# Router gate folded into the two projections of an attention and mixture-of-experts kernel, with all attention stages in a new order

## The reference

```
x: (8, 512, 128) float32; 4096 tokens of 128 numbers
x = x + attention(layernorm(x)); x = x + experts(layernorm(x))
attention: Q, K, V = n @ W.T + b, 16 heads of 8; scores = Q K^T, causal mask, no softmax
           out = (scores * causal) V;  return out @ wo.T + bo
experts:   probs = softmax(n2 @ Wg) over 8 experts; the top 2 of each token
           y = sum over the two of p * (relu(n2 @ W1[e] + b1[e]) @ W2[e] + b2[e])
```

## Time and profile before

| | |
|---|---|
| median of 3 runs (range) | 298.18 us (297.58 to 298.75) |
| the profiled execution, its own time | 297.89 us |
| its span in the trace | 296.1 us |
| busy: PE, DVE, ACT, POOL | 228.8, 201.2, 142.4, 204.5 us |
| mean granted TensorE clock | 0.899 of 2.4 GHz |

### The profile page before, as it was taken

The page is one execution under the profiler, slowest core; times in us unless marked ns, Lnnn a source line. Parts: engine busy times, 40 slices in busy tenths (PEclk is TensorE's granted clock), DMA queues, the critical chain, the costliest instruction groups (busy, mean ns, idle before and its releaser), DMA issues.

```text
span 296.1 us, 6311 instructions
## 1 busy us (share of the span) xinstructions
PE 228.8 (77%) x1392; PEld 171.2 (58%) x1392; DVE 201.2 (68%) x696; ACT 142.4 (48%) x509; POOL 204.5 (69%) x188
## 2 busy tenths in 40 slices
PE   0499999999999998988794399999997999840000
PEld 0244666666656565655573279988996989830000
DVE  7978889889898998989967485454443544410284
ACT  3234366646476463654444156666664757510000
POOL 3166568738889889889776777777777777777000
PEclk9999999999999999999955569999999999985555
DMA  6940000000100100100115532343333333211599
GB/s 203 312 101 0 0 3 0 3 1 20 38 26 29 39 27 28 38 27 28 49 53 114 132 101 74 98 111 97 97 104 98 106 97 104 82 49 34 184 358 309
DMA packets 32357, 24.98 MB, mean 84 GB/s; under 512 B 4388, under 2 KB 30252, under 8 KB 32322
## 3 DMA queue, kind: packets, MB, share of 16 engines
q1 hardware_dynamic: 23766, 14.01, 17.8%
q0 software_dynamic: 4320, 8.47, 8.8%
q10 hardware_dynamic: 4236, 2.10, 2.4%
HBM read 13.41 MB, written 11.61 MB: 84 GB/s over the span
## 4 chain that ended last, share of the span: by engine, by line
PE 49%; DVE 16%; issue 11%; DMA 11%; POOL 5%; ACT 2%; SPq 2%; ACTq 1%; POOLq 1%; DVEq 0%
PE ps L820 15%; PE ps L790 7%; PE ps L909 6%; PE ps L917 6%; POOL returned L397 5%; DMA returned<-y_sb,xt 4%; DMA back<-returned 4%; DVE o_sb L590 3%; DVE prod L577 3%; DMA xt<-dispatched 2%; PE ps L811 2%; PE ps L829 2%; SPq L323 2%; PE ps L840 2%; PE ps L792 2%
## 5 line engine op out<-in xcount | busy, mean ns | idle before, releaser
L397 POOL DMA_INDIRECT returned<-y_sb,xt x71 | 70.2, 989 | 21.7 <-issue 17.4
L358 POOL TENSOR_TENSOR outer<-qkv 128x1024 f32<-128x1024 f32 x32 | 62.5, 1954 | 27.3 <-ACT qkv L452 26.9
L388 POOL DMA_INDIRECT dispatched<-rows,slot x64 | 62.6, 978 | 18.9 <-issue 14.5
L820 PE MATMUL ps<-outer,causal 128*128 128x512 f32 x128 | 63.1, 616 | 0.0
L766 DVE TENSOR_SCALAR y_sb<-ps,xt 128x128 f32<-128x128 f32 x71 | 24.9, 350 | 45.3 <-PE ps L919 45.3
L909 PE MATMUL ps<-xT,w_of 128*128 128x128 f32 x284 | 48.7, 295 | 1.6 <-ACT xT L502 1.1
L917 PE MATMUL ps<-w_sb,hT 128*128 x284 | 44.7, 281 | 0.5 <-DVE y_sb L766 0.4
L508 ACT ACTIVATE hT<-ps,b_col 128x128 f32<-128x128 f32 x142 | 44.3, 365 | 0.9 <-PE ps L909 0.7
L577 DVE TENSOR_TENSOR prod<-ps,qkv 128x1024 f32<-128x1024 f32 x32 | 39.0, 1220 | 4.7 <-PE ps L820 4.7
L909 PEld LDWEIGHTS ps<-xT,w_of 128*128 128x128 f32 x284 | 38.5, 197 | 3.8 <-ACT xT L502 2.8
L590 DVE TENSOR_REDUCE o_sb<-prod 128x128 f32<-128x1024 f32 x32 | 38.7, 1210 | 0.1
(11 more groups left out here) (140 smaller groups left out, 385.7 us busy)
## 6 DMA issues: line engine op xcount, KB each, us to landing
xt<-dispatched SPq DMA_DIRECT2D x71, 65.0 KB, 1.9
back<-returned SPq DMA_DIRECT2D x8, 512.0 KB, 7.4
x_sb<-x SPq DMA_DIRECT2D x8, 256.0 KB, 4.6
out<-x_sb ACTq DMA_DIRECT2D x8, 256.0 KB, 6.6
returned<-y_sb,xt POOLq DMA_INDIRECT x71, 2.3
w_sb<-w SPq DMA_DIRECT2D x1, 1024.0 KB, 6.4
w_sb<-w SPq DMA_DIRECT2D x2, 512.0 KB, 7.4
dispatched<-rows,slot POOLq DMA_INDIRECT x64, 2.3
```

What stands on the lines that cost most here:

```text
L358: pool.tensor_tensor(outer[:, g % OUTER_RING, :].rearrange("p (h b a) -> p h b a", h=HEADS, b=DH), k, v, ALU.mult).then_inc(outer_done, 1)
L388: pool.indirect_dma_start(out=dispatched[:, :], out_offset=bass.IndirectOffsetOnAxis(ap=slot[:, g * K + k:g * K + k + 1], axis=0), in_=row ...
L397: pool.indirect_dma_start(out=returned[:, :], out_offset=bass.IndirectOffsetOnAxis(ap=xt[:, n % G, D:D + 1].bitcast(I32), axis=0), in_=y_s ...
L820: mm = pe.matmul(ps_run[g % 2][:, u, :], causal[:, :], outer[:, g % OUTER_RING, 512 * u:512 * (u + 1)], start=True, stop=True)
```

## The change

The router's logits of normalized x2 are those of x2 with the mean taken out, times 1/deviation; x2 is x plus the attention's output. The change computes (x - mean) @ Wg from two places: eight more columns on the Q, K, V projection (times x's own deviation, `std1`) and eight more on the output projection. Wg is centred once by a matmul with I - 1/128, and wo and bo are multiplied by it once. The logits are added up on DVE, and 1/deviation goes in as the scale of the exponential, one per tile. A row carries the exponential and the reciprocal of the sum, and `y_out` multiplies by both. `shift2_out` moves from DVE to ACT as two instructions, `transpose2`, `xn2T_out` and `gate` go, the one-hot choice becomes eight `tensor_scalar` from SBUF in place of one `tensor_tensor` that read PSUM, and every engine's list is written anew. PSUM regions move: the projection gets bank 7, the output projection and the logits bank 0.

```diff
             load_x(0).then_inc(x_in[0], 16)
-            sp.dma_start(wqkv_sb[:, :], w_qkv).then_inc(w_qkv_in, 16)
+            sp.dma_start(wg_sb[:, :], w_gate).then_inc(w_g_in, 16)
+            sp.dma_start(wqkv_sb[:, 0:3 * D], w_qkv).then_inc(w_qkv_in, 16)
             load_x(1).then_inc(x_in[1], 16)
-            sp.dma_start(wo_sb[:, :], w_o).then_inc(w_o_in, 16)
+            sp.dma_start(wo_sb[:, E:ATT], w_o).then_inc(w_o_in, 16)
+            sp.dma_start(w_o_rows_sb[:, :], w_o_rows).then_inc(w_o_in, 16)
+            sp.dma_start(b_o_col[:, :], b_o.rearrange("(d one) -> d one", one=1)).then_inc(w_o_in, 16)
...
-            tile_slots([(16, dispatch), (0, outer_product), (0, split_bias)], N)
+            tile_slots([(10, dispatch), (0, outer_product), (0, split_bias)], N)
...
+                act.activation(std1[:, own.start:own.stop], log1[:, own.start:own.stop], ACT.Exp, scale=0.5).then_inc(std1_done, 1)
...
+            def negative_mean2(g):
+                wait(act, stats2_done, g + 1)
+                act.activation(negmean[:, g:g + 1], mv2[:, g, 0:1], ACT.Identity, scale=-1.0).then_inc(negmean_done, 1)
+
+            def shift2_out(g):
+                wait(act, rstd2_done, g + 1)
+                wait(act, negmean_done, g + 1)
+                act.activation(norm2[:, g, 1:2], norm2[:, g, 0:1], ACT.Identity, scale=negmean[:, g:g + 1]).then_inc(norm2_done, 1)
...
+                act.activation(gx[:, g, :], ps_qkv[:, 3 * D:PROJ], ACT.Identity, scale=std1[:, g:g + 1]).then_inc(gx_done, 1)
...
-                act.activation(expd[:, :, :], shifted[:, :, :], ACT.Exp).then_inc(exp_done, 1)
+                for u in range(T):
+                    act.activation(expd[:, u, :], shifted[:, u, :], ACT.Exp, scale=norm2[:, g + 1 - T + u, 0:1]).then_inc(exp_done, 1)
...
-            tile_slots([(10, variance_log2), (12, exponentials), (10, scale2_out), (2, qkv_out), (11, xn2T_out), (1, xnT_out), (6, qT_out), (10, rows_out),
-                        (0, normalize), (7, oT_out), (0, deviations_ahead)], N)
+            act.wait_ge(gate_mm, 1)
+            act.activation(wqkv_sb[:, 3 * D:PROJ], ps_gate, ACT.Identity).then_inc(gate_done, 1)
+            tile_slots([(7, shift2_out), (2, qkv_out), (5, oT_out), (1, xnT_out), (0, normalize), (6, variance_log2), (6, scale2_out),
+                        (6, exponentials), (4, qT_out), (7, rows_out), (6, negative_mean2), (0, deviations_ahead)], N)
...
+                dve.tensor_tensor(ps_lg, ps_lg, gx[:, b * T:(b + 1) * T, :], ALU.add).then_inc(logits_done, 1)
...
-                wait(dve, expert_done, 1)
-                if g + STATE_AFTER < N:
-                    wait(dve, kv_done, states(g + STATE_AFTER))
-                dve.tensor_tensor(pick[:, :, :, :], top_i[:, :, 0:K].unsqueeze(3).to_broadcast([P, T, K, E]),
-                                  ps_expert.unsqueeze(1).unsqueeze(1).to_broadcast([P, T, K, E]),
-                                  ALU.is_equal).then_inc(pick_done, 1)
+                dve.tensor_copy(top_f[:, :, :], top_i[:, :, 0:K]).then_inc(topf_done, 1)
+                wait(dve, ids_done, 1)
+                dve.tensor_copy(rows[:, g + 1 - T:g + 1, :, D + 1], top[:, :, 0:K]).then_inc(chosen_done, 1)
                 wait(dve, gsum_done, b + 1)
-                dve.reciprocal(grec[:, :], gsum[:, :]).then_inc(grec_done, 1)
...
+                dve.reciprocal(rows[:, g + 1 - T:g + 1, :, D + 2], gsum[:, :].unsqueeze(2).to_broadcast([P, T, K])).then_inc(chosen_done, 1)
+                wait(dve, topf_done, b + 1)
                 for u in range(T):
-                    dve.tensor_scalar(rows[:, g + 1 - T + u, :, D + 1], top[:, u, 0:K], grec[:, u:u + 1], None,
-                                      ALU.mult).then_inc(chosen_done, 1)
+                    for k in range(K):
+                        dve.tensor_scalar(pick[:, u, k, :], expert_no[:, :], top_f[:, u, k:k + 1], None, ALU.is_equal).then_inc(pick_done, 1)
...
+            def gate_bias(g):
+                if g != 0:
+                    return
...
-            tile_slots([(6, stats2_out), (6, mean2_out), (5, add_residual), (9, softmax_end), (1, attend_sum),
-                        (8, softmax_start), (0, attend), (0, scales_ahead), (9, places), (6, shift2_out),
-                        (2, state_out), (EARLY_AFTER, early_table)], N)
+            tile_slots([(0, gate_bias), (0, scales_ahead), (0, state_out), (2, attend_sum), (1, attend), (5, places), (3, add_residual), (3, stats2_out),
+                        (4, softmax_end), (3, mean2_out), (3, softmax_start), (EARLY_AFTER, early_table)], N)
...
+            def gate_weights(g):
+                if g != 0:
+                    return
+                pe.wait_ge(gate_done, 1)
+                pe.wait_ge(w_o_in, 3 * 16)
+                pe.matmul(ps_gate_o, w_o_rows_sb[:, :], wqkv_sb[:, 3 * D:PROJ], start=True, stop=True)
+                pe.matmul(ps_gate_b, b_o_col[:, :].to_broadcast([P, P]), wqkv_sb[:, 3 * D:PROJ], start=True, stop=True).then_inc(gate_o_mm, 1)
...
-            tile_slots([(3, running_sums), (11, gate), (5, q_transposed), (7, o_transposed), (5, sum_state), (1, project),
-                        (0, transpose1), (10, transpose2), (7, project_out), (12, rank)], N)
+            pe.wait_ge(center_done, 1)
+            pe.wait_ge(w_g_in, 16)
+            pe.matmul(ps_gate, center[:, :], wg_sb[:, :], start=True, stop=True).then_inc(gate_mm, 1)
+            tile_slots([(5, project_out), (1, project), (1, sum_state), (7, rank), (0, transpose1), (4, o_transposed), (2, running_sums),
+                        (3, q_transposed), (0, gate_weights)], N)
```

More of the change, by code:

```diff
@@ L384, in dispatch @@
                 wait(pool, rows_done, g + 1)
-                wait(pool, chosen_done, g + 1)
+                wait(pool, chosen_done, 2 * batches(g - g % T + T - 1))
                 apart(pool)
@@ L720, in final_table @@
                                   ALU.add, ALU.min).then_inc(table_done, 1)
+            dve.wait_ge(ident_done, 1)
+            dve.tensor_scalar(center[:, :], ident[:, :], -1.0 / D, None, ALU.add).then_inc(center_done, 1)
             mean1_out(0)
```

150 lines of the change are left out of this document (83 added, 67 removed).

## The result

The changed kernel takes 308.32 us (median of 4 runs, 306.61 to 310.81); the kernel before takes 297.88 (median of 4, 297.55 to 298.75). The ratio is 1.0346, with an interval of 1.0307 to 1.0386: 3.5% slower, where 293.4 us was forecast and 299.0 was the end of the range. The profiled execution took 308.58 us, with a span of 306.80 and a granted clock of 0.887.

The account below looks back on a forecast made before the run. POOL alone was taken to set the end from 69.25 us on. The shorter lag's 7.0 us, less 2.5 us of standing in the drain, start send-backs 4.5 us sooner: 297.89 becomes 293.4 us, range 289.0 to 299.0.

Parts of the forecast that it names:

- What bounds the kernel: From 69.25 us on POOL alone sets the end; PE and DVE matter only for its first dispatch and last slots.
- POOL's ledger: Kernel before: from 69.25, 16 slots of 4.42 us, 16 tiles of 2.53 and about 2 of waits give 182.5.
- The lag, 7 us: POOL's dispatch 10 instead of 16 behind the outer product: send-backs could start at 175.5 instead of 182.55, 7.0 us sooner.
- The start, outer product 9 at 45.9: POOL's start of outer product 9: 42.65 before, plus 0.45, 2.3 and 0.3 us gives 45.7, taken as 45.9.
- I leave the 0.8 that is already in DVE's busy time: DVE standing behind POOL's outer product: kept at 0.8 us per batch, though the port rule allowed up to 1.95.
- The price of that rule, 0.2 x 5.5 batches = 1 us: If DVE stood a whole outer product, 1.1 us more takes it to 17.9 of 17.7 per batch, adding 1 us.
- Rival C: Attention loop stretches past POOL at DVE's softmax_end and PE's transpose1; at 4.8 us per slot 301.8 us; chance 0.13.
- 2 us of PE standing per batch, 17 of 17.7: PE in the loop: about 15 us of work plus some 2 us standing per batch, 17 of POOL's 17.7.
- The drain, slots at t+17.7 after the last outer product: Last batch's slots ready 17.7 us after the last outer product ends, at 167.9; POOL stands 2.5 us.
- The end, 22.0 us: After the send-backs: reading back, adding and storing take 22.0 us, unchanged.
- D: A wash: slots stretched by 0.1 to 0.25 us or a late first dispatch; 296.5 to 299 us; chance 0.14.
- B: The drain hides: last batch's slots are there by 165.4, giving 290.9 us, or 289.5 at best; chance 0.23.

Follow-up runs that it names:

- section 5: The runs c3, e14, e15 and e16, on a chip where the kernel before takes 298.04 us; they took 294.06 to 307.25 us.
- e16: e14 with a dispatch lag of 16 outer products instead of 10: 301.68 us, 1.0118 of the kernel before.
- e14: Changed kernel with one SBUF tensor_tensor for the cast and eight comparisons, and a reduction for the copy of the exponentials: 294.06 us, 0.985 of the kernel before.
- c3: The changed kernel unaltered, as control on a chip where the kernel before takes 298.04 us: 307.25 us, 1.0297 of it.
- e7: Changed kernel with DVE's statistics ahead of the choice, and rank, slots and dispatch one slot later: 344.52 us, 1.013 of the kernel before on a slower chip.
- e15: e14 with the early table made in DVE's slot 25 instead of in the drain: 295.84 us, 0.9925 of the kernel before.
- e1: Changed kernel with the choice as one tensor_tensor against PSUM and the exponentials copied by a reduction: 334.15 us, 0.9835 of the kernel before on a slower chip.
- e2: e1 with the plain SBUF-to-SBUF copy of the exponentials kept: 335.23 us, 0.9841 of the kernel before on a slower chip.
- c1: The changed kernel unaltered, as control on a slower chip: 344.06 us, 1.0038 of the kernel before there.
- e12: The same form as e14, run on a slower chip: 335.13 us, 0.9766 of the kernel before there.
- e13: e12 with a dispatch lag of 16 instead of 10, on a slower chip: 343.82 us, 1.0019 of the kernel before there.

## Why the prediction was wrong, step by step

- **What bounds the kernel**: right. POOL's ledger holds in every run of section 5, and 1.29 us per send-back too.
- **The lag, 7 us**: right, 6.8 us at the first send-back, 6.7 without POOL's waits (`e16` against `e14`).
- **The start, outer product 9 at 45.9**: 1.4 us too early for the new lists themselves (47.26 in `e14`, 0.5 us of standing included), the rest of the 3.2 is the choice of batch 0 (0.77 us for the cast and 1.83 for the comparisons, beside a bias split of POOL from 44.36 to 45.41; PE's next transpose then waits 0.82 us for qT).
- **"I leave the 0.8 that is already in DVE's busy time"**: this step failed. The earlier trace rows showed 0.8 us of standing in four instructions, and the length of the eight comparisons was put at 0.6 to 1.2 us, rightly (1.1, and 1.3 with the cast). But their standing was 2.3 us per batch, not 0.8. The 0.8 was what was left of an outer product that had begun 1 us before the four. Timeline of POOL before:

```profile
93.80 1.97 POOL L358 TENSOR_TENSOR outer<-qkv 128x1024 f32<-128x1024 f32 x1
```

  The new lists bring the choice to the start of one (104.50 and 104.68). The Trainium skill (SBUF — State Buffer, "Who interferes with whom") says that the engine that comes second waits for the other's whole instruction. The cast of 2.17 us that ended with the outer product agrees in its length, though by the records it began 0.18 us before it, and the 5.57 us of `e7` show that it can happen twice in a row. The traces show the standing and what ends it, not what lies between the two engines.
- **The price of that rule, 0.2 x 5.5 batches = 1 us**: failed as well, and is the deeper fault. I set the standing against DVE's average load per batch. What it meets is a chain within one slot: choice, `picked` and statistics, PE's rank and ACT's logarithm, qT, transpose, qkv, 2.76 us from the end of the choice to the outer product. POOL waited 7.4 us in the loop; the last slots came 2.3 us later in the drain, and some 2 us went at the start. Rival C named this mechanism and its place, at 0.13; its 301.8 us took in the loop only, not the later start and the longer drain.
- **"2 us of PE standing per batch, 17 of 17.7"**: the average was near, and just as beside the point: in `e14` PE doesn't stand for `picked` in the loop at all, only in the drain (5.76 us at 166.59), in the changed kernel 16.9 us in six stands over the whole, 6.8 of them in the drain.
- **The drain, slots at t+17.7 after the last outer product**: t+16.5 in `e14` (151.83 to 168.29), t+20.0 in the changed kernel, whose batch 6 came out of the loop behind.
- **The end, 22.0 us**: 24.2 in the first profile, 22.4 in `c3`, 23.4 in `e14`, 22.0 in `e15`. It scatters between executions; an effect of the change on it isn't shown.
- **D and B**: neither happened; PE's savings were worth nothing by themselves, as said.

## What to carry to other kernels

When a change adds many small SBUF-to-SBUF instructions on DVE beside long GpSimd work, price each batch of them at one whole GpSimd instruction, add the length of those that still come behind it, and put that on the chain that hangs on them, not on DVE's average load. Look in the trace for a small instruction that ends exactly with another engine's long one. One comparison in place of a cast and eight comparisons took this kernel from 1.030 to 0.985 of the old time, and it is worth a run to see where in the other engine's rhythm it falls.

## What the runs showed of the hardware that was not expected

- The cast of 128 x 8 began 0.18 us (104.50) and 0.68 us (103.67) before the record of the outer product with which it ended, while POOL's dispatch was running. The tensor_tensor of `e14` at 99.50, inside a dispatch that another dispatch followed, took 0.17. Whether the dispatch or the start of the outer product holds DVE there stays open.
- While POOL multiplied or split a bias (batches 0 and 1), a reduction over an axis of length one copied the exponentials in 0.17 us where the plain copy in the same place took 0.77 and 2.60 (`e1`, `e2`); a tensor_tensor with two SBUF operands did stand (up to 2.53 us), that with one in PSUM never did (208 ns on average over 8 in `e1`, four of them during an outer product).
- On three chips the same kernels take 12 to 15% longer. POOL's send-backs wait for DVE's `y_sb` there (37.9 us in `c1`), and DVE stands up to 8.0 us at a time (`e12`), ACT up to 8.9 (`e7`) and once 17.7 (`e13`), where the profile names no instruction or DMA of this core as the cause ("remote" or "issue"). Timeline of DVE in `e12`, the drain:

```profile
167.00 0.29 DVE L586 TENSOR_TENSOR x_sb<-ps,x_sb 128x128 f32<-128x128 f32 x1 [7.97 <-remote]
```

What sets these chips apart from the others was not looked into. The difference between the chips moved the ratio of the changed kernel from 1.030 (`c3`) to 1.004 (`c1`), so a change should be judged on the kind of chip for which it was forecast.
